# Four gated layers: gate table in fp32, first activations ahead of the gates, transfers in another order, and shifted scores ten steps behind the maxima

## What is computed

```python
x = x + tanh(g_xattn[L]) * xattn_L(layernorm(x), ctx, ctx)
x = x + tanh(g_ffn[L]) * ffn_L(layernorm(x))
```

```python
h = act(x[t] @ W1[e] + b1[e])
out[t] += gate[t, e] * (h @ W2[e] + b2[e])     # gate is 0 where e is not chosen
```

## Time and profile before

| | |
|---|---|
| Time, three runs | 663.67, 665.51, 665.88 us; median 665.51 |
| Profiled execution | 666.34 us, span 664.5, mean granted PE clock 0.966 |
| PE busy | 597.9 us (90%) |
| DVE busy | 503.4 us (76%) |
| ACT busy | 362.7 us (55%) |
| POOL busy | 225.1 us (34%) |
| Layer 0 experts | 58 to 140 us |
| Layer 1 attention, experts | 147 to 229, 242 to 300 |
| Layer 2 experts | 378 to 482 |
| Layer 3 attention, experts | 498 to 588, 603 to 659 |

### The profile page before, as it was taken

The page is one execution under the profiler, slowest core; times in us unless marked ns, Lnnn a source line. Parts: engine busy times, 40 slices in busy tenths (PEclk is TensorE's granted clock), DMA queues, the critical chain, the costliest instruction groups (busy, mean ns, idle before and its releaser), DMA issues.

```text
span 664.5 us, 11727 instructions
## 1 busy us (share of the span) xinstructions
PE 597.9 (90%) x3413; PEld 437.8 (66%) x3437; DVE 503.4 (76%) x1287; ACT 362.7 (55%) x639; POOL 225.1 (34%) x438
## 2 busy tenths in 40 slices
PE   8898699977999878998999799999996999987996
PEld 5684588746776556874666557888764777654784
DVE  6857779979776357987753579999969788545896
ACT  6326345524666614553566157888833665632885
POOL 4211255422101113532112027898730000111793
PEclk9989989999999979999999899999999999997999
DMA  8224886210000005711001127777310000000771
GB/s 286 63 95 145 180 196 174 75 49 1 5 27 3 26 1 130 183 32 33 5 5 41 33 78 249 238 234 242 107 33 1 3 28 3 3 0 9 251 244 45
DMA packets 33134, 59.06 MB, mean 89 GB/s; under 512 B 6530, under 2 KB 22562, under 8 KB 33084
## 3 DMA queue, kind: packets, MB, share of 16 engines
q1 hardware_dynamic: 32508, 57.43, 29.4%
q10 hardware_dynamic: 576, 1.02, 0.4%
HBM read 53.61 MB, written 4.29 MB: 87 GB/s over the span
## 4 chain that ended last, share of the span: by engine, by line
PE 66%; DVE 17%; ACT 5%; issue 5%; SPq 3%; DMA 3%; POOL 1%; DVEq 0%; ACTq 0%
PE PS L734 11%; PE PS L735 10%; PE PS L736 10%; PE PS L982 5%; PE PS L890 4%; PE PS L965 4%; PE PS L572 3%; DVE negmax L1684 2%; DVE consts L1690 2%; PE PS L997 2%; DVE qst L1644 2%; DVE hid_lo L1590 1%; PE PS L962 1%; PE PS L938 1%; DVE PS L1584 1%
## 5 line engine op out<-in xcount | busy, mean ns | idle before, releaser
L475 POOL TENSOR_TENSOR wpair<-ring,ones_col 128x128 fp32r<-128x128 f32 (+1 forms) x150 | 88.5, 590 | 148.1 <-PE PS L736 123.3
L1268 ACT ACTIVATE pT<-PS 128x512 f32<-128x512 f32 x160 | 92.3, 593 | 50.8 <-PE PS L965 41.5
L1590 DVE TENSOR_TENSOR hid_lo<-PS,hid_hi 128x512 fp32r<-128x512 f32 x150 | 102.3, 682 | 1.8 <-ACT hid_hi L1176 1.3
L1176 ACT ACTIVATE hid_hi<-PS 128x512 fp32r<-128x512 f32 x150 | 89.2, 594 | 18.6 <-DVE PS L1584 18.1
L477 POOL TENSOR_TENSOR wpair<-ring,wpair 128x128 fp32r<-128x128 f32 (+1 forms) x150 | 88.1, 587 | 11.7
L734 PE MATMUL PS<-xhi,wpair 128*128 128x512 f32 x204 | 85.6, 420 | 6.3 <-POOL wpair L477 5.2
L735 PE MATMUL PS<-xlo,wpair 128*128 128x512 f32 x204 | 82.9, 406 | 0.0
L736 PE MATMUL PS<-xhi,wpair 128*128 128x512 f32 x204 | 82.5, 404 | 0.0
L1170 ACT ACTIVATE pT<-PS,ring 128x512 f32<-128x512 f32 x96 | 66.0, 690 | 18.4 <-PE PS L736 17.3
L890 PE MATMUL PS<-kz,qst 128*128 128x256 f32 x256 | 59.7, 317 | 11.5 <-DVE negmax L1690 7.1
L734 PE MATMUL PS<-hid_hi,wpair 128*128 128x512 f32 x150 | 62.5, 417 | 6.7 <-DVE hid_lo L1590 6.5
(11 more groups left out here) (239 smaller groups left out, 1117.1 us busy)
## 6 DMA issues: line engine op xcount, KB each, us to landing
qst<-gates SPq DMA_DIRECT2D x42, 512.0 KB, 4.8
qst<-gates SPq DMA_DIRECT2D x42, 256.0 KB, 4.2
ring<-in_mlp SPq DMA_DIRECT2D x48, 128.5 KB, 3.1
ring<-in_glu SPq DMA_DIRECT2D x27, 192.0 KB, 4.4
kz<-keys SPq DMA_DIRECT2D x36, 96.0 KB
keys<-qst SPq DMA_DIRECT2D x6, 512.0 KB, 3.7
qst<-kfull SPq DMA_DIRECT2D x96, 4.0 KB
wq<-in_wq SPq DMA_DIRECT2D x3, 256.0 KB, 3.5
```

The source lines that it names most:

```text
L475: pool.tensor_tensor(wpair[:, pair, 0, c], w, ones, ALU.mult).then_inc(M["wstep"], 1)
L1176: act.activation(hid_hi[:, kept, :], PS[:, gate_bank(glu, kept), :], ACT.Copy).then_inc(M["hi"], 1)
L1268: act.activation(pT[:, w % 8, :], PS[:, 2 + w % 2, :], ACT.Exp, scale=sc).then_inc(A["p"], 1)
L1590: dve.tensor_tensor(hid_lo[:, kept, :], PS[:, gate_bank(glu, kept), :], hid_hi[:, kept, :].bitcast(f32), ALU.subtract).then_inc(M["lo"], 1)
```

## The change

1. **Gate table.** No bf16 parts: eight fp32 transposes of 32 × 128 (L734 in the changed kernel), two copies of 32 × 512 (half 0 by DVE, half 1 by ACT), spreads as fp32 matmuls over 32 rows (L775), the bias as one fp32 matmul a half (L809) behind an empty one that opens the bank (L807). One DMA saves the table. `BY_PE` is 2: four spreads, and `first_gates` fetches two entries.
2. **First activations.** They are taken before the gates are there (two in gated layers, four in MLP layers), into `oT` and `kfull`. In MLP layers `up` runs four units ahead, and later activations stay in PSUM, where DVE multiplies them by the gates.
3. **Residuals.** Layer 0's term is added by POOL (`add_tokens`), layer 2's by PE, as the identity times x in two parts (L814). POOL waits for the table before it goes on to the third split.
4. **Transfers.** In layer 0 the refills come right behind the first gates, and the window copies, masks and key blocks one group behind each of the refills 4 to 8. Layer 2's keys are computed at the end of layer 1's attention, and saved and stacked in layer 1's experts ahead of the refills.
5. **Attention, layers 1 and 3.** LAG is 10; the queries of half 1 at steps 12, 16, 20, 24; the fourth product of half 0 and the norm's second half are inside the loop; turns, copies and outputs are moved to other steps.
6. **Filler.** `keep_busy` ahead of the turn is (0, 2, 8, 4) in place of (0, 13, 22, 10), and 15 in place of 8 at the end of attentions 2 and 3; two fillers in the loop are gone.

```diff
-        BY_PE = 3
+        BY_PE = 2
...
-        LAG = 14
+        LAG = 10
         NU = B * H
         NUW, LAGW = 2 * B * NW, 10
-        Q_AT = (4, 5, 8, 9)
+        Q_AT = (12, 16, 20, 24)
...
-                    sp.wait_ge(rows_out, L + 1)
-                    for j in range(4):
-                        sp.dma_start(gd[L].rearrange("e (a j n) -> j e a n", a=NHALF, j=4)[j],
-                                     gate_rows[EP * j:EP * (j + 1), :].rearrange("e (a n) -> e a n", a=NHALF)).then_inc(rows_saved, 16)
+                    sp.wait_ge(rows_out, NHALF * (L + 1))
+                    sp.dma_start(gd[L].rearrange("e (a n) -> e a n", a=NHALF), gate_rows[:, :, :]).then_inc(rows_saved, 16)
 
                 def first_gates():
-                    sp.wait_ge(rows_saved, 64 * (L + 1))
+                    sp.wait_ge(rows_saved, 16 * (L + 1))
...
-                if L == 0:
-                    flag_keys()
-                    save_keys(1)
-                    save_keys(3)
-                    stack_keys(1, range(KSLOTS))
-                    save_gates()
-                    save_keys(2)
-                    shift_windows()
-                    for K in (1, 3):
-                        sp.wait_ge(k_saved[K], 48)
-                    first_gates()
...
+                if L == 0:
+                    flag_keys()
+                    save_keys(1)
+                    save_keys(3)
+                    save_gates()
+                    for K in (1, 3):
+                        sp.wait_ge(k_saved[K], 48)
+                    first_gates()
+                    for e in range(RING, n):
+                        refill(e, e - RING, e % RING)
+                        if e == RING:
+                            shift_windows()
+                        elif e == RING + 1:
+                            sp.wait_ge(ac["kfreq"], 2)
+                            sp.dma_start(mask_i[:, 0, :, :], t["mask_q"]).then_inc(ld_mask, 16)
+                            sp.dma_start(mask_i[:, 1, :, :], t["mask_k"]).then_inc(ld_mask, 16)
+                        elif e < RING + 2 + KSLOTS:
+                            stack_keys(1, (e - RING - 2,))
+                    return
+                if L == 2:
+                    stack_keys(3, range(KSLOTS))
+                save_gates()
+                first_gates()
+                if L == 1:
+                    save_keys(2)
+                    stack_keys(2, range(1))
...
+                def add_tokens(i):
+                    pool.tensor_scalar(xn[:, i, :], xn[:, i, :], gzero[:, i:i + 1], None, ALU.mult).then_inc(topped, 1)
+                    pool.wait_ge(topped, 2 * i + 1)
+                    pool.tensor_tensor(x[:, i, :], x[:, i, :], xn[:, i, :], ALU.add).then_inc(topped, 1)
...
+                        pool.wait_ge(rt["tab"], L + 1)
+                    elif L == 0:
+                        add_tokens(e - 1)
...
-                for hf in range(NHALF):
-                    pe.transpose(PS[:, 1, S + hf * P:S + (hf + 1) * P],
-                                 wtab[:, 4 * hf:4 * hf + 4, :].rearrange("p t e -> p (t e)"), ident)
-
-            def turn_weights(L):
-                pe.wait_ge(rt["parts"], L + 1)
                 for i in range(NT):
-                    mm = pe.transpose(PS[0:PARTS * EP, 1 - i // 4, (i % 4) * 64:(i % 4 + 1) * 64].bitcast(bf16),
-                                      wpart[:, i, :, :].rearrange("p a e -> p (a e)"), identb[:, :])
-                mm.then_inc(rt["tr"], 1)
+                    mm = pe.transpose(PS[0:EP, 6 + i // 4, (i % 4) * P:(i % 4 + 1) * P], wtab[:, i, :], ident)
+                    if i % 4 == 3:
+                        mm.then_inc(rt["tr"], 1)
...
-                if L > 0:
-                    keep_busy(0, (0, 13, 22, 10)[L])
+                    pe.wait_ge(rt["shift"], 1)
+                    for half in (KV_LN, KV_LN + 1):
+                        key_value(half)
+                    for half in (KV_LN, KV_LN + 1):
+                        key_rest(half)
+                keep_busy(0, (0, 2, 8, 4)[L])
+                if not glu:
+                    for u in (2, 3):
+                        up(u, 1, 1, u % 2)
                 turn_rows(L)
-                turn_weights(L)
-                pe.wait_ge(rt["wT"], 2 * (L + 1))
+                pe.wait_ge(rows_out, NHALF * (L + 1))
+                if L == 0:
+                    pe.wait_ge(astep, 1)
+                for u in range(2 if glu else KEPT):
+                    spread(u, u // 2, u, first=True)
+                if L == 0:
+                    pe.wait_ge(kv_out, KV_LN + 2)
                 for hf in range(NHALF):
-                    if hf == 1:
-                        pe.wait_ge(rows_out, L + 1)
-                    if glu:
-                        mm = pe.matmul(PS[:, hf, :], zerob[:, 0:P], zerob[:, :], start=True, stop=False,
+                    mm = pe.matmul(PS[:, hf, :], zerob[:, 0:P], zerob[:, :], start=True, stop=False, skip_group_check=True)
+                    if not glu:
+                        mm = pe.matmul(PS[:, hf, :], b2[L][:, :], gate_rows[:, hf, :], start=False, stop=False,
                                        skip_group_check=True)
-                    else:
-                        for j in range(PARTS):
-                            mm = pe.matmul(PS[:, hf, :], b2part[L][:, j, :], wT[:, hf * HALF:(hf + 1) * HALF],
-                                           start=(j == 0), stop=False, skip_group_check=True)
+                    if L == 2:
+                        pe.wait_ge(set_dve, 3)
+                        for part in (xhi, xlo):
+                            mm = pe.matmul(PS[:, hf, :], eye[:, :], part[:, hf * HALF:(hf + 1) * HALF], start=False, stop=False,
+                                           skip_group_check=True)
                     mm.then_inc(M["y"], 1)
...
                 def loop():
                     for p in range(NU + LAG):
-                        if p in (2, 3):
-                            keep_busy(6, 2)
                         if p < NU:
                             max_scores(p)
+                        if p == 1:
+                            project_queries(0, HGRP - 1, 2 + HGRP - 1)
+                        if p == 2:
+                            layer_norm(2 * L, (1,))
                         if p in Q_AT:
-                            project_queries(1, Q_AT.index(p), 4 + Q_AT.index(p) % 2)
-                        if p % 4 == 2 and 0 <= (p - 6) // 4 < 4 * B:
-                            turn_max((p - 6) // 4)
+                            project_queries(1, Q_AT.index(p), 7)
                         w = p - LAG
                         if w >= 0:
                             shifted_scores(w)
                             if w >= 5 and w % 4 == 1:
                                 weigh_values(*divmod((w - 5) // 4, 4))
-                            if w >= H and w % H in (6, 7, 12, 13):
-                                turn_outputs(w // H - 1, w % H // 12, w % 6 % 2)
+                            if w >= H and w % H in (5, 9):
+                                for pair in range(2):
+                                    turn_outputs(w // H - 1, w % H // 9, pair)
+                        if p % 4 == 1 and 0 <= (p - 5) // 4 < 4 * B:
+                            turn_max((p - 5) // 4)
...
-                keep_busy(5, 8)
+                if L == 1:
+                    for n in (KV_LN + 2, KV_LN + 3):
+                        key_value(n)
+                    for n in (KV_LN + 2, KV_LN + 3):
+                        key_rest(n)
+                else:
+                    keep_busy(5, 15)
...
+                early = 2 if glu else KEPT
+                for u in range(early):
+                    unit(u, u // 2, u % KEPT, first=True)
+                if L == 0:
+                    for half in (KV_LN, KV_LN + 1):
+                        key_high(half)
+                    for half in (KV_LN, KV_LN + 1):
+                        key_low(half)
+                act.wait_ge(rt["tr"], NHALF * (L + 1))
+                act.activation(gate_rows[:, 1, :], PS[0:EP, 7, :], ACT.Copy).then_inc(rows_out, 1)
                 for u in range(2 * RING):
...
-                dve.tensor_copy(wpart[:, :, 0, :], wtab[:, :, :]).then_inc(rt["tab"], 1)
-                dve.wait_ge(rt["tab"], L + 1)
-                link(dve.tensor_tensor(wrest[:, :, :], wtab[:, :, :], wpart[:, :, 0, :], ALU.subtract))
-                link(dve.tensor_copy(wpart[:, :, 1, :], wrest[:, :, :]))
-                dve.tensor_tensor(wpart[:, :, 2, :], wrest[:, :, :], wpart[:, :, 1, :], ALU.subtract).then_inc(rt["parts"], 1)
...
-                dve.wait_ge(rt["tr"], L + 1)
-                dve.tensor_copy(wT[:, HALF:N], PS[0:PARTS * EP, 0, 0:S].bitcast(bf16)).then_inc(rt["wT"], 1)
-
-                def add_input(i):
-                    if L == 0:
-                        link(dve.scalar_tensor_tensor(out=x[:, i, :], in0=xn[:, i, :], scalar=gzero[:, i:i + 1],
```

(24 more changed lines are left out.)

215 lines of the change are left out of this document (103 added, 112 removed).

## The result

| | before | changed |
|---|---|---|
| Median (lowest to highest), six runs each | 664.66 (663.28 to 667.15) us | 659.92 (657.71 to 660.76) us |
| Ratio, 95% interval | | 0.9917 (0.9899 to 0.9936) |
| Profiled execution, span | 666.34, 664.5 us | 657.71, 655.9 us |
| Mean granted PE clock | 0.966 | 0.949 |

The change makes the kernel faster by 0.8%, which is more than 0.3%, but the time lies above the range of 641 to 656.5 and 12 us above the forecast. The page of the changed kernel: span, busy time by engine, the chain that ended last, the clock in 40 slices, and two groups.

A forecast was written before the change was run, and what follows sets the result against it. TensorE (PE) was taken to hold two thirds of the path. Terms −10.0 − 2.7 + 1.5 − 2.4 − 4.1 = −17.7 took 666.34 to 648.6, or 647.8 us on the median's scale; 8-in-10 range 641 to 656.5.

The forecast's parts named there:

- Layer 0, experts: Layer 0's experts: the stall ahead of up(8) and the idle time before the slow clock disappear, −10.0 us (−12 to −4).
- granted clock 1.0 from 62 on: Sign to look for in layer 0: PE at full clock from 62 us, without an idle stretch over 1 us.
- the slow start goes: Layer 2's experts: the first units take 1.34 us each in place of 1.70, −2.9 us.
- fit, barely: Layer 0: key copies behind refills 6 to 8 fit, SP needing 3.7 us of about 4.1 an entry.
- Rival (b): Layer 0's stall stays in part, refill(5) held by SP's copies or units by DVE: half the term, 653 us; chance 0.14.
- Attention, −2.7 and −4.1 by forecast: Layers 1 and 3: shifting ten behind starts shifted scores sooner, less dearer steps and products: −2.7 and −4.1 us.
- Rival (a): Attention: the copy of the maxima comes late at ten behind; slower outcome, chance 0.05; mild form, 654 us, 0.12.
- Layer 1, experts: Layer 1's experts: SP's longer queue delays refill(4), PE stalls 3 us before up(8): +1.5 us (−1.8 to +5).
- Rival (c): Layer 1's queue is worse, a stall with half clock, +3.5 us more: 651 us; chance 0.12.
- Layer 2, −2.4 by forecast: Layer 2's experts: earlier rows, ups in place of filler and quicker units against +3.7 of PE: −2.4 us (−0.5 to −5).
- Layer 3, 0: Layer 3's experts: rows 1.4 us sooner and two early ups against +2.7 of PE: −0.1, called 0.
- Rival (d): DVE, not PE, holds the MLP units, so most of 5.6 us freed on DVE is won: 643 us; chance 0.09.

The follow-up runs named there:

- experiment 3: The changed kernel with spreads and bias products over 128 rows, and layer 1's twelve key copies behind layer 0's last refill: 642.85 us, ratio 0.9686.
- experiment 8: As experiment 3, plus three empty 128-row matmuls behind each of the two down-projections before the last in gated layers: 641.84 us, ratio 0.9671.
- experiment 1: The changed kernel with its spreads and bias products over 128 rows in place of 32, the added rows zero: 647.25 us, ratio 0.974.
- experiments 2 and 6: The kernel before with filler ahead of the turn in layers 1 to 3 over 32 rows (675.48 us), and with the change's attention part alone (657.41 us).

## Why the prediction was wrong, step by step

**The step that failed** is in *Layer 0, experts*, and was used again in layers 2 and 3: that with the idle stretches gone the clock would be full ("granted clock 1.0 from 62 on"; "the slow start goes"). The prediction took PE's idle time as what lowers the clock, counted the new spreads and bias products as busy time, and priced what stands behind them at full clock. It priced the fp32 products rightly: 0.86 to 0.94 us by forecast, 3.70 / 4 = 0.93 at full clock. But that price came from products over all 128 rows (`128*8` in the earlier trace rows), and that the new ones use 32 was taken to mean nothing for the clock. The spreads and bias products of before use 96 rows, in bf16, so no row of its trace showed several us of work over 32. What the runs showed in its place: over 32 rows the clock is half for 10 us in layer 2 and 7 in layer 3, with PE busy all along, and in layer 0 it takes until 67 to come back. With 128 rows, and nothing else changed, the time is 647.25 us, where 647.8 was forecast. That agreement is partly luck, as the terms show.

**Layer 0, −10.0 by forecast, −6.4 measured.** The timeline of the changed kernel, first spreads and behind them the SP queue:

```profile
55.71 2.47 PE L775 MATMUL PS<-pT,ctx_tok 32*128 32x512 f32 x4 [0.68 <-ACT pT L1217]
...
58.59 0.99 PE L744 MATMUL PS<-xhi,wpair 128*128 128x512 f32 x1
...
67.93 0.50 PE L744 MATMUL PS<-hid_hi,wpair 128*128 128x512 f32 x1
```

```profile
62.69 0.58 SPq L393 DMA_DIRECT2D ring<-in_glu  x1
```

The start was better than forecast. The table was turned at 53.99 where 56.5 was taken, up(2) came at 58.59 and not 60.6, and refill(4) at 62.69 and not 64.5. The stall of the earlier trace rows is gone, as forecast. Then the two units with a spread took 5.05 and 5.09 us at half clock, where 2.2 and 2.9 had been summed (six and nine products and a spread), so that up(8) came at 76.92 and not 73.9. The second step, that the key copies "fit, barely" among the refills, counted SP's issue time (3.7 of 4.1 us an entry) and left out the DMA engines, whose share was already 1.03 in the earlier trace rows. In the changed kernel the slow clock hid that error; with 128 rows it appeared as the stop at 95 and cost 3.6 us. Rival (b), that layer 0's stall stays in part, is what happened with 128 rows. The key copies that it named held a ring load, but a later one than refill(5), and through the engines' share and not SP's queue. Without both errors the stage is 12.3 us shorter than before (experiment 3), just past the forecast's outer bound of −12.

**Behind layer 0, not in the sum, +1.5.** Half clock from 132 to 139. The prediction had no term for it and needed none: it comes and goes between executions of the same program (experiment 8).

**Attention, −2.7 and −4.1 by forecast, −2.6 and −4.1 measured.** First query product, first shifted score and last weighing, in layer 1 and in layer 3:

```profile
142.76 0.50 PE L883 MATMUL PS<-xhi,wqpair 128*128 128x512 f32 x1
...
154.34 0.63 PE L987 MATMUL PS<-qst,kz 128*128 128x256 f32 x2
...
219.79 1.07 PE L1004 MATMUL PS<-pT,vall 128*32 128x256 f32 x16 [0.94 <-ACT pT L1307]
...
486.52 0.50 PE L883 MATMUL PS<-xhi,wqpair 128*128 128x512 f32 x1
...
500.38 0.99 PE L987 MATMUL PS<-qst,kz 128*128 128x256 f32 x2
...
576.34 1.07 PE L1004 MATMUL PS<-pT,vall 128*32 128x256 f32 x16 [0.71 <-ACT pT L1307]
```

The first shifted score of layer 1 is 11.6 us behind the first query product, against 18.25 before: −6.7, where −5.4 was forecast. The 64 steps behind it take 65.45 us, 1.02 each against 0.96, which is +4.1 where +2.7 was summed. So two errors of 1.3 us cancel, and the exact hit of layer 1's term is luck. Layer 3 went the same way: 13.9 us to the first shifted score against 21.1, −7.3, then 75.96 us for 64 steps, 1.19 against 1.14 each, +3.2. Rival (a), maxima copied too late, did not come: in the changed kernel the shifted scores (L987) idled 2.9 us in all their 256 matmuls, and the releaser was ACT.

**Layer 1, experts, +1.5 by forecast, −1.8 measured.** SP, POOL and PE around the first refill:

```profile
250.26 3.35 SPq L350 DMA_DIRECT2D kz<-keys  x4
253.73 0.44 SPq L393 DMA_DIRECT2D ring<-in_glu  x1
```

```profile
256.30 0.61 POOL L479 TENSOR_TENSOR wpair<-ring,ones_col 128x256 fp32r<-128x256 f32 x1 [3.35 <-DMA ring<-in_glu]
```

```profile
257.89 0.40 PE L744 MATMUL PS<-xhi,wpair 128*128 128x512 f32 x1
```

The queue is as forecast, with four key copies of 3.35 us ahead of the refill. Counted from the last weighing, the refill is issued at 33.9 us where 35.3 was summed, mostly since the table was out a microsecond sooner. And the load landed in 2.6 us, not the 4.4 of the median, so that POOL had the split done at 257.7, just ahead of PE's 257.89. There is no stall. The term failed mainly in the size of one landing: the median is mostly of loads that share the engines with gate rows, and this one was issued when they had little to do (share 0.44 from 252 to 255). The margin is thin. In experiment 1 PE waits 1.48 us for the split at this place (256.71), so the wait that the forecast saw is real and only its size was off. Rival (c), with a half clock on top, came in neither.

**Layer 2, −2.4 by forecast, +2.6 measured, −3.9 with 128 rows. Layer 3, 0, +2.2 and −1.8.** The units are quick from the second one on (1.36 us, where 1.34 was forecast), so the mechanism of the term, DVE freed of the residual, was right. The half clock from 381 to 391 and from 603 to 610 is most of the difference between the last two figures: from the turn to the first down-projection it cost 5.2 of 6.5 us in layer 2 and 3.3 of 4.0 in layer 3. Why with 128 rows both layers came out 1.5 and 1.8 us better than forecast is not accounted for, beyond the microsecond by which executions differ. Rival (d), DVE holding the units, had the right effect and not the consequence. DVE's product with the gates takes 696 ns in all 134 where 84 took 757, and POOL's split 444 ns where it took 590, but the units didn't get shorter, as PE was the bound.

**The chances.** 0.92 stood on faster by over 0.3%, and so it is. The range was built from the bounds of the terms, and each bound was computed at full clock. It had no case for a clock lowered by the change's own new matmuls, which was worth 10.5 us in layers 2 and 3 alone, more than rivals (b) and (c) together (5.2 and 3.2 by their own times).

## What to carry to other kernels

Read the rows of a matmul in the profile before pricing what stands behind it: here several us of products over 32 rows left TensorE at 1.2 GHz although it never paused, and padding the contraction with zeros to 128 rows made no product longer and gave some 12 us. When transfers are moved among others, sum the load of the DMA engines in the new place and not just the issuing queue's time, and put what isn't needed soon behind the last urgent one. When a fix gives nothing, look in the trace whether the wait that it removes was there at all: an earlier loss may have hidden it, as layer 0's slow start hid the late ring load.

## What the runs showed of the hardware that was not expected

- The granted clock was 0.50 with PE busy for 4.00 of 4.00 us, in fp32 products over 32 rows and in bf16 filler over 32 rows. The same filler over 128 rows brought it to 1.00, and the same fp32 products over 128 rows, 96 of them zeros, kept it there in layers 2 and 3. The fp32 spreads cost 0.92 us at full clock with 32 rows or 128.
- The four such spreads of layer 1 left it at 1.00; the same four in layer 0 ran at 0.50, and no run tells why.
- The same waits of 1.09 and 0.93 us, in kernels with the same program up to there, were followed by a clock of 0.50 in one execution and 1.00 in another (experiments 2 and 6, from 136 to 140 us).
- With the DMA engines' share at 1.06 they moved 233 GB/s in layer 0's experts (gate rows in broadcast, ring loads, key copies). A ring load was then so late that POOL waited 3.87 us for it, 12.5 us after its issue.
- A 192 KB ring load landed in 2.6 us where little was in flight ahead of it, against a median of 4.4 in the kernel before and 5.7 in the changed one, in which most of them share the engines with gate rows.
